# Second attention of a two-layer kernel: two-part output summed on leaving PSUM, projection over 256 rows, first batch's rows placed earlier

## The reference, cut to what matters

```python
q, k, v = qkv[0], qkv[1], qkv[2]
q = rmsnorm(q, q_norm_w)
k = rmsnorm(k, k_norm_w)
scores = jnp.einsum('bhqd,bhkd->bhqk', q, k) * scale
attn = jax.nn.softmax(scores, axis=-1)
out = jnp.einsum('bhqk,bhkd->bhqd', attn, v)
out = out.transpose(0, 2, 1, 3).reshape(B, L, dim)
return jnp.einsum('bld,ed->ble', out, w_proj) + b_proj
```

## Time and profile before

| | |
|---|---|
| median of 3 runs | 1404.0 us (1403.33 to 1404.58) |
| the profiled execution's own time | 1404.14 us |
| its span (first to last instruction) | 1402.3 us |
| mean granted TensorE clock | 0.997 |
| busy over the span: TensorE, VectorE, ScalarE, GpSimd | 96%, 65%, 54%, 53% |
| second layer | from about 890 us to the end |

### The profile page before, as it was taken

One profiled execution on the slowest core, in us unless ns is written; L12 is line 12 of the kernel. 1 busy time (PEld: TensorE's weight loads), 2 busy tenths in 40 slices (PEclk: granted clock), 3 DMA queues, 4 the chain that ended last, 5 costly groups with the idle time before them and its releaser, 6 DMA issues. The chain is left out here.

```text
span 1402.3 us, 25300 instructions
## 1 busy us (share of the span) xinstructions
PE 1349.8 (96%) x8758; PEld 1201.7 (86%) x8758; DVE 910.4 (65%) x1793; ACT 752.8 (54%) x1948; POOL 738.1 (53%) x725
## 2 busy tenths in 40 slices
PE   9999899999999999999999999879999999999898
PEld 7887798999899989998999898668888888889797
DVE  6655566556656665666565665557887777786765
ACT  4553444545544555445544544246666666666664
POOL 1651333554444545434645453448658676866775
PEclk9999999999999999999999999999999999999999
DMA  5995333324332343233324424166555653645572
GB/s 191 328 329 201 83 91 93 89 77 121 106 89 49 102 138 92 62 90 104 106 65 119 119 65 170 67 173 188 145 177 162 188 173 105 205 149 168 174 196 90
DMA packets 105645, 190.78 MB, mean 136 GB/s; under 512 B 20304, under 2 KB 39440, under 8 KB 103216
## 3 DMA queue, kind: packets, MB, share of 16 engines
q1 hardware_dynamic: 105520, 189.17, 45.0%
HBM read 116.68 MB, written 30.47 MB: 105 GB/s over the span
## 5 line engine op out<-in xcount | busy, mean ns | idle before, releaser
L775 POOL TENSOR_TENSOR a_pr<-a_pr,a_ri 128x512 f32<-128x512 f32 x128 | 133.2, 1041 | 299.5 <-DVE a_ri L955 299.5
L832 ACT ACTIVATE a_pr<-a_score,a_nb 128x256 f32<-128x256 f32 x256 | 119.0, 470 | 267.6 <-DVE a_nb L947 267.6
L1376 POOL TENSOR_TENSOR l_pr<-l_pr,l_ri 128x512 f32<-128x512 f32 x128 | 133.2, 1040 | 121.5 <-DVE l_ri L1728 119.5
L1487 ACT ACTIVATE l_pr<-l_score,l_nb 128x256 f32<-128x256 f32 x256 | 119.1, 471 | 107.7 <-DVE l_nb L1696 107.6
L58 PE MATMUL a_job<-s_xs,s_wh 128*128 128x512 f32 x384 | 153.8, 401 | 1.0 <-PEq L221 1.0
L60 PE MATMUL a_job<-s_xs,s_wl 128*128 128x512 f32 x384 | 151.7, 395 | 0.0
L59 PE MATMUL a_job<-s_xs,s_wh 128*128 128x512 f32 x384 | 151.3, 394 | 0.0
L947 DVE TENSOR_REDUCE a_nb<-a_score 128x2 f32<-128x512 f32 x128 | 88.5, 691 | 85.8 <-PE a_score L1026 84.1
L1696 DVE TENSOR_REDUCE l_nb<-l_score 128x2 f32<-128x512 f32 x128 | 87.5, 684 | 39.4 <-PE l_score L1836 39.2
L960 DVE TENSOR_TENSOR a_pt<-a_turn,a_pt 128x512 fp32r<-128x512 f32 x128 | 87.5, 684 | 23.7 <-ACT a_pt L840 23.7
L1495 ACT ACTIVATE s_wh<-l_turn 128x512 fp32r<-128x512 f32 x128 | 76.9, 600 | 36.3 <-PE l_turn L1846 36.3
(11 more groups left out here) (251 smaller groups left out, 4569.2 us busy)
## 6 DMA issues: line engine op xcount, KB each, us to landing
s_wl<-wgu_scratch SPq DMA_DIRECT2D x56, 512.0 KB, 5.7
a_sk<-a_rotk SPq DMA_DIRECT2D x384, 64.0 KB, 2.0
a_sq<-a_rotq SPq DMA_DIRECT2D x256, 64.0 KB, 2.0
s_xs<-xn_scratch SPq DMA_DIRECT2D x14, 1024.0 KB, 5.7
l_wd<-wd_scratch SPq DMA_DIRECT2D x56, 256.0 KB, 2.9
l_zq<-qs_scratch SPq DMA_DIRECT2D x128, 64.0 KB, 4.3
l_sk<-ks_scratch SPq DMA_DIRECT2D x32, 256.0 KB, 4.9
a_raw<-in_w SPq DMA_DIRECT2D x30, 256.0 KB, 3.0
```

What stands on the lines that cost most here:

```text
L775: pool.tensor_tensor(e, e, ri[:, n % 2, :].unsqueeze(2).broadcast_to([P, 2, SEQ]), ALU.mult)\
L832: i = act.activation(pr[:, n % 2, t, :], PS[n % 2][:, t * SEQ:(t + 1) * SEQ], ACT.Exp, bias=nb[:, n % 2, t:t + 1], accum_out=sm[:, n % 2, ...
L1376: pool.tensor_tensor(e, e, ri[:, n % 3, :].unsqueeze(2).broadcast_to([P, 2, SEQ]), ALU.mult)\
L1487: i = act.activation(pr[:, n % 3, t, :], PS[n % NPS][:, t * SEQ:(t + 1) * SEQ], ACT.Exp, bias=nb[:, n % 3, t:t + 1], accum_out=sm[:, n % 3 ...
```

## The change

- `vp` is laid out anew: the high parts of a group of four heads lie in rows 0 to 63 of `PO`, the low parts in rows 64 to 127.
- When a group is done, ScalarE copies one half of `PO` across to the other half's partitions of a buffer `ol` (`out_low`), and VectorE adds the other half to it (`out_sum`) into 64 rows of a float32 buffer `os`; even groups fill rows 0 to 63, odd ones 64 to 127. This frees `PO`.
- After every second group ScalarE makes the high part of `os` (`out_hi`, slots 10, 18, 26, ...), and GpSimd the low part (`out_lo`, same slots, behind that slot's normalise).
- The projection runs over 2 blocks of 128 rows: 12 matmuls a batch. Its weights are half as large, in one DMA; one piece less is prepared in the first stage.
- The planner counts P at 6 units, the goal of a slot is 28.1; X stands last in its slot, in every batch; for the first batch X is in slots -9 and -8 (before -7 and -6), and the work before it and the first two stack loads are moved forward.

```diff
-VG, VSTRIDE, VBLK = 4, 160, 640
+VG, VB, VSTRIDE, VBLK = 4, 2, 144, 576
+VHALF = VG * D1
...
-                for i in range(2):
-                    sp.dma_start(l1.wp[:, :, 2 * i:2 * i + 2]...
+                sp.dma_start(l1.wp.bitcast(F32).rearrange("p s a d -> p s (a d)"), wp_dram[0]).then_inc(l1.w_in, 16)
...
-    T, Q, V, S_, P_, LOG, CMB, GU, DH = 4, 12, 12, 4, 12, 20, 4, 12, 6
+    T, Q, V, S_, P_, LOG, CMB, GU, DH = 4, 12, 12, 4, 6, 20, 4, 12, 6
...
-    UNIT, SLOT_GOAL, EARLY_GOAL = 10, 28.7, 18
+    UNIT, SLOT_GOAL, EARLY_GOAL = 10, 28.1, 18
...
-        return (9, 10)
+        return (7, 8) if m == 0 else (9, 10)
...
+        ITEMS[n].sort(key=lambda item: item[0][0] == "X")
...
+    LOAD_AT = {2 * PER_LOAD * i - 4 if i > 1 else i - 6: i for i in range(N // (2 * PER_LOAD))}
...
-                    if n % (2 * PER_LOAD) == 0 and 0 <= n // (2 * PER_LOAD) + 1 < N // (2 * PER_LOAD):
-                        load_stack(n // (2 * PER_LOAD) + 1)
+                    if n in LOAD_AT:
+                        load_stack(LOAD_AT[n])
...
+                def out_lo(k):
+                    pool.wait_ge(S["out_hi"], k + 1)
+                    pool.tensor_tensor(ot[:, 1, k % VB, :], os[:, k % VB, :], ot[:, 0, k % VB, :], ALU.subtract).then_inc(S["out_lo"], 1)
...
-                        if u in (4, 5, 6):
-                            root_rms(b + 1, u - 4)
-                        if u == 8:
+                        first_root = 3 if b < 0 else 4
+                        if u in (first_root, first_root + 1, first_root + 2):
+                            root_rms(b + 1, u - first_root)
+                        if u == (5 if b < 0 else 8):
                             weigh(b + 1)
...
                         normalise(n + 1)
+                    if n >= 10 and (n - 10) % 8 == 0 and (n - 10) // 8 < VB * BATCH:
+                        out_lo((n - 10) // 8)
...
-                def out_hi(g):
+                def out_low(g):
+                    here, there = VHALF * (g % 2), VHALF * (1 - g % 2)
                     act.wait_ge(S["pv_done"], 4 * g + 4)
-                    if g >= VG:
-                        wait_full(act, ("P1", g // VG - 1))
-                    act.activation(ot[:, 0, g % VG, :], PO[:, 0:SEQ], ACT.Copy).then_inc(S["out_hi"], 1)
+                    act.activation(ol[here:here + VHALF, :], PO[there:there + VHALF, 0:SEQ], ACT.Copy).then_inc(S["out_low"], 1)
+
+                def out_hi(k):
+                    act.wait_ge(S["out_free"], 2 * k + 2)
+                    if k >= VB:
+                        wait_full(act, ("P1", k // VB - 1))
+                    act.activation(ot[:, 0, k % VB, :], os[:, k % VB, :], ACT.Copy).then_inc(S["out_hi"], 1)
...
                     if n >= 6 and (n - 6) % 4 == 0 and (n - 6) // 4 < VG * BATCH:
-                        out_hi((n - 6) // 4)
+                        out_low((n - 6) // 4)
                     if 0 <= n + 1 < N:
                         exps(n + 1)
+                    if n >= 10 and (n - 10) % 8 == 0 and (n - 10) // 8 < VB * BATCH:
+                        out_hi((n - 10) // 8)
...
-                def out_lo(g):
-                    dve.wait_ge(S["out_hi"], g + 1)
-                    dve.tensor_tensor(ot[:, 1, g % VG, :], PO[:, 0:SEQ], ot[:, 0, g % VG, :], ALU.subtract).then_inc(S["out_free"], 1)
+                def out_sum(g):
+                    here = VHALF * (g % 2)
+                    dve.wait_ge(S["out_low"], g + 1)
+                    if g >= 4:
+                        dve.wait_ge(S["out_lo"], (g - 4) // 2 + 1)
+                    dve.tensor_tensor(os[here:here + VHALF, g // 2 % VB, :], PO[here:here + VHALF, 0:SEQ], ol[here:here + VHALF, :], ALU.add)\
+                       .then_inc(S["out_free"], 1)
...
-                        if u in ((4, 5) if b < 0 else (2, 3)):
-                            sum_squares(b + 1, u - (4 if b < 0 else 2))
+                        if u in (2, 3):
+                            sum_squares(b + 1, u - 2)
...
-                        if u in (7, 8):
-                            scale_rows(b + 1, u - 7)
+                        first_scale = 4 if b < 0 else 7
+                        if u in (first_scale, first_scale + 1):
+                            scale_rows(b + 1, u - first_scale)
...
-                        pe.wait_ge(S["out_free"], VG * (m + 1))
-                        for a in range(VG):
+                        pe.wait_ge(S["out_lo"], VB * (m + 1))
+                        for a in range(VB):
...
-    rows = [[(VG * a + p // (2 * D1)) * D1 + p % D1 for p in range(P)] for a in range(VG)]
+    rows = [[(2 * VG * j + p // D1) * D1 + p % D1 for p in range(P)] for j in range(VB)]
```

## The result

| | before | after |
|---|---|---|
| median of the runs (us) | 1404.3 (1403.33 to 1404.79) | 1423.14 (1421.47 to 1425.91) |
| ratio, with its 95% interval | | 1.0135 (1.0119 to 1.015) |
| the profiled execution: time, span | 1404.14, 1402.3 | 1421.47, 1419.7 |

The account below looks back on a forecast made before the run. TensorE, busy 428 of 448 us, was taken as the bound, with VectorE near enough to stop it for moments. Terms -9.9 + 9.2 - 4.9 + 0 - 0.9 = -6.5 us against 1404.1 gave 1397.6 us, range 1388 to 1405.

Parts of the forecast that it names:

- The projection's matmuls: Inside the slots of seven batches, 84 fewer projection matmuls on TensorE at 0.118 us each: -9.9 us.
- What the halves cost: The output's added steps on ScalarE (6.3 us) and GpSimd (11.9 us) lie off the path as work: 0.
- The wait in front of P0: In seven batches P0 waits 1.7 us in the mean for GpSimd's `out_lo`: 12.0 us, less 2.8 absorbed, net +9.2.
- X last: X, put last in its slot, no longer waits for its scaled rows: -4.9 us, bounds -4.9 and 0.
- The planner: The new goal only spreads the same feed-forward pieces over the slots, ending in slot 128 and not 129; no price.
- The start: In the second layer's first batch, TensorE's idle time moves from the first scores to later products: 0, bounds -7.2 and +4.
- rival 1: The layer's start gets shorter as its name says, 7.2 us less than forecast: 1390.4 us; chance 0.14.
- The end: After the last values, four output steps cost +0.5 us and 12 fewer matmuls save 1.4: -0.9 us, bounds -1.4 and +0.5.
- The rule on the shared port: GpSimd's 16 added steps could lock VectorE out of SBUF: up to 12 us more by the skill, 0 by the rows.
- The third: Rival: the matmuls' gain is all paid back and X's turns into VectorE waits: 1402.5, up to 1404 us; chance 0.14.
- the fourth: Rival: P0's wait makes the kernel slower, 19 us and not 9.2, from a mean wait of 2.6 us: 1407.4; chance 0.12.

Follow-up runs that it names:

- The half projection: The kernel before with each projection summed over only two of the four groups, 96 matmuls fewer, lists untouched: 1401.48 us, ratio 0.9975.
- the doubled one: The changed kernel with X first, old start, goal 28.2, `out_lo` ahead of the normalise, and each projection product issued twice: 1409.16 us, ratio 1.0031.
- the old lists: The new output on the lists of the kernel before (P at 12, goal 28.7): 1405.78 us with `out_lo` ahead of the normalise, 1415.37 us behind it.
- the rest undone: The changed kernel with X first, old start and goal 28.2: 1416.68 us; with `out_lo` also ahead of the normalise: 1404.26 us.

## Why the prediction was wrong, step by step

**The projection's matmuls, -9.9 us: the step that failed.** "All of it lies on the engine that sets the time" was inferred from TensorE's 96% busy. The half projection gives 3 us, the doubled one 5. A busy TensorE is not a bound by itself: behind P0 the turn came just when VectorE's low part was ready. The row that could have told this is the first of the earlier trace rows: 25 waits on VectorE mean a pair of engines that take turns in being last, and matmuls taken from such a slot count only up to the next of these waits. The forecast used that row for X's and P0's terms, and not here. That the rest of the 11.3 us is hidden behind VectorE is read from the turn's waits, which move by 6 us in either direction.

**What the halves cost, 0: failed by 4.3 us.** "Off the path: ScalarE idles a third of the stretch" read a mean over the stretch. The copy stands ahead of a chain of read-outs in one slot, where ScalarE has no idle time. Of the 5.3 us between the two profiled executions 2.5 lie in the slots u = 11 and 2.2 in u = 3. The first is shown by moving the copy; that the second is the same copy at u = 2 rests on the same pattern in the traces and was not tried. Another 1.7 are in the tail and belong to the term of the end, and the rest of the trace gives 1.1 back.

**The wait in front of P0, +12.0 in the waits, +9.2 net: right.** 13.4 us in seven waits, 2.43 us in slot 19; taken out it was worth 9 us on the changed kernel, 9.6 on the old lists, 12.4 with the rest undone. That the net comes out near 9.2 is partly luck: what I let go for the catching up of the turn (2.8 us) is 3.6 to 5.8 us in the waits, and the low clock behind some of P0's waits, for which the forecast had nothing, makes up for it.

**X last, -4.9 us: wrong sign.** The forecast named the case, "if VectorE's late X job only turns into a wait of the next turn", and took the other end of the bound "as the row names X itself". Alone it costs 3 us: the turn pays 6.0 us for the 4.5 that X saves, and in the first batch, which the term left out, X last delays the stack and the first scores. A wait's row names where the lateness ends, not whether it is gone if the waiter moves.

**The planner, no term.** "The new goal only spreads the same pieces" was the step without a price. D0 of tile 14 went from last in slot 28 to first in slot 29, ahead of which `y_sum` must be done, and 3.6 us of wait with the slow clock behind it made the slot 5.3 us longer. That this piece is the cause is shown by goal 28.2, where the wait is gone and slots 29 to 31 are 6.0 us shorter.

**The start, 0: right in its mechanism, short in size.** The C store at 925.54 (forecast 925.1), first scores at 926.23 without a wait (927.4), tile 5's product waiting instead, the weights at 934.07 (932 to 933). "TensorE idles just as long" was 7.45 us and not 5.0, since TensorE came there sooner and the data did not; alone the step costs 2 us. The gain of rival 1 is nowhere.

**The end, -0.9: +1.5.** From slot 125 on 26.7 us against 25.2. P0 comes 0.6 us later behind the last values, as the four steps were priced, and the 12 matmuls save 1.35 between P0's first and P1's last. But up to the last values the tail takes 1.3 us more: the down products end in slot 128 as forecast, so that none lie between the last turn and its values any more, and there TensorE waits 0.94 us for VectorE. From P1's last matmul to the end it is 5.7 us and not 4.8, with one of VectorE's last steps beside GpSimd's (1.22 us, 0.69 before).

**The rule on the shared port.** It priced up to 12 us. L1635's multiplies, 16.3 us of VectorE before, are 18.9 us after (L1652, 16 each); but none of them runs beside an `out_lo`, the GpSimd steps next to the long ones are others. Beside 15 of the 16 `out_lo` VectorE's steps keep their length. The last one, in the tail, shows the case itself:

```profile
1411.15 1.83 DVE L1705 SCALAR_TENSOR_TENSOR l_y<-l_yt,l_y 128x512 f32<-128x512 f32 x2
...
1412.39 1.74 POOL L1400 TENSOR_TENSOR l_y<-l_y,l_s 128x512 f32<-128x512 f32 x1
```

Two such steps took 1.29 us before; here the second, which starts beside `out_lo` (1411.65 to 1412.43), takes 1.22 of the 1.83. The Trainium skill (SBUF — State Buffer, the section on its two separate sides) has VectorE and GpSimd exclude each other where both read SBUF, VectorE with two inputs. The trace agrees for this pair, and `out_sum`, with one input in PSUM, kept its 0.417 us (0.429 at most, 12 of 32 beside GpSimd). So the added GpSimd steps cost VectorE 0.5 us in all, and not 12.

**The rivals.** None had this time. The third was nearest in kind (the gain paid back, X's waits turned into VectorE's) and priced at 1402 to 1404; the fourth put P0's mean wait at 2.6 us or more, and it was 1.9. What was missing is that the parts add: a gain not had (5 to 7 us), X (8), the copy (4, with its share of the tail), slot 29 (5), start and end (2 to 4), some 24 to 28 us where 25.5 lie between forecast and result. These prices come from different kernels, and waits shift between the parts, so the agreement proves little. By place, in the two profiled executions, it is firmer: the start 1.7 us (forecast 0), slot 29 5.3 (none), the other slots up to 125 8.8 (-9.9 + 9.2 - 4.9 = -5.6), the tail 1.5 (-0.9). More than half of the miss, 14.4 us of 24, lies in those other slots, where the matmuls' and X's terms stood.

## What to carry to other kernels

Before matmuls are counted as a gain, look at what ends the next wait behind them; where a second engine is late every few slots, take them out in a trial and measure that first. An added short step on an engine that idles a third of the time is free only at the place where it idles: read that engine's timeline in that slot, above all what stands behind the step. And when a planner's cost or goal is touched, compare its lists item by item: one piece across a hand-over cost 5.3 us here, and 11.3 us of matmuls gave 3 to 5.

## What the runs showed of the chip that I had not expected

Idle times of 3.6 us (slot 29) and 7.45 us (the start) were each followed by matmuls at a granted clock well under full, 0.63 over 4.61 us in the first case; one of 2.6 us in the tail came with a mean clock of 0.77 over the last 29 us. Slot 29 became 5.3 us longer for a wait of 3.6. Waits of P0 of 2.0 to 2.5 us were followed by 0.50 in some slots and not in others, and not in the same ones in every execution: none of the seven in the changed kernel's, three in the one with goal 28.2, two with `out_lo` last on the old lists. The executions of one kernel differ in the same way: with the old start three took 1423.0 to 1423.7 us at mean clocks of 0.990 to 0.992, the fourth 1419.8 at 0.995. The store of C's result (8 x 512 float32) that SyncE issued at 925.54 let its queue go on only at 928.14, 2.6 us later, and the loads of weights behind it waited as long.
